# Graph attention, one core: the layer norm's 1/std multiplied in at the projection's eviction, rows centred by VectorE for 24 tiles, and nodes added to stored results in the tail

## The chip, the cores and the metric

One Trainium2 chip, one of its cores. The time is that of one launch on the device, in microseconds. Times inside the program come from one profiled execution and are counted from its first instruction.

## What is computed

`x` has 6144 nodes of 512 features, `adj` is a 6144 x 6144 matrix of 0 and 1 (int32), thinly filled. There are 8 heads of 64 features.

```python
h = maximum(layernorm(x), 0)              # (x - mean) / sqrt(var + 1e-5), no weights
g = einsum('ni,hif->hnf', h, W)           # projection, 8 heads
s1, s2 = einsum('hnf,hf->hn', g, a1), einsum('hnf,hf->hn', g, a2)
scores = leaky_relu(s1[:, :, None] + s2[:, None, :], 0.2)
scores = where(adj > 0, scores, -9e15)
att = softmax(scores, -1)
out = x + elu(transpose(einsum('hnm,hmf->hnf', att, g)))
```

## The kernel before

The nodes are cut into 48 tiles of 128. There are two stages, each a block in which every engine runs its own list of instructions, tied by semaphores.

**Stage 1, `project_and_scan` (L496, up to about 340 us).** Per tile t: VectorE takes the moments of the row (`moments`, L559, bn_stats), GpSimd adds them up (`spread`, L724), ScalarE takes the square root (`deviation`, L637), VectorE the reciprocal (`scale`, L564), GpSimd makes the shift (`offset`, L737), and ScalarE writes relu(x / std + shift) in one ACTIVATE (`norm`, L642, L647). TensorE transposes it (`turn`, L684), ScalarE copies the transpose out of PSUM (`turned`, L650), TensorE multiplies with W and the folded score weights (`project`, L693), and ScalarE copies the three results out (`h_out`, L656, L661 to L663). SP stores the finished rows in a table in DRAM and loads the next x rows (six buffers) and adjacency rows, all on one queue (L542 to L555). The first 30 adjacency tiles are scanned beside this: each half tile (1.5 MB, `load_adj`, L241, six buffers) is packed by ScalarE (`pack`, L253, 2.9 us), and VectorE looks for the largest entries (L263, L274, L295, L297). The plan `spread_over` (L355) deals the scan's work over the 48 rounds by estimated cost; ScalarE's packs stand in the round before VectorE's first step of their tile, mostly two in a round. ScalarE's order in round t is: `turned(t)`, `norm(t + 1)`, the first pack, `h_out(t - 1)`, `deviation(t + 3)`, the other packs. TensorE's is `turn(t + 1)`, `project(t)`. VectorE's is `moments(t + 3)`, `scale(t + 2)`, then its scan. `normed` and `normedT` have two buffers.

SP also copies x into the output for tiles 0 to 21, two tiles (512 KB) at a time, in rounds 2 to 22 (`copy_nodes`, L215, L220): 11 DMAs from DRAM to DRAM.

**Stage 2, `attend_edges` (L768).** 33 units (one or two tiles, or a part of one), in 29 groups that end in a result. GpSimd gathers table rows by index (L904, L909), 6 to 10 indirect DMAs of 128 rows per unit, up to three units ahead of VectorE (`AHEAD`) and as a ring of 36 row buffers allows. VectorE scores the edges (`score_edges`, L1136, the first step is L1141), ScalarE takes the exponential, VectorE weighs the rows (L1156), TensorE adds them up, VectorE normalises (L1168), ScalarE does the negative side of elu (`grow`, L965), VectorE finishes it (`finish`, L1173). The last 18 adjacency tiles are scanned beside units 0 to 18. `result` has four buffers.

What happens to a finished result depends on its tile. Groups 0 to 15 (tiles 0 to 21) "lie in the output": GpSimd adds them to the copied x by an accumulating DMA from SBUF to DRAM (`add_x`, L888), issued after the gathers of the unit four later. Groups of tiles 22 to 43 get x added in SBUF by an accumulating DMA (L890), and ScalarE stores them (`store`, L973, L979), four units later. For the last four tiles x is loaded beforehand, VectorE adds it, and SP stores.

## Time and profile before

| | us |
|---|---|
| Three runs | 772.21, 772.41, 775.91; median 772.41 |
| The profiled execution | 777.28 |
| Its span, first to last instruction | 775.6 |
| Busy: TensorE / VectorE / ScalarE / GpSimd | 575.2 / 651.3 / 477.7 / 422.4 |
| DMA moved | 269.50 MB, mean 347 GB/s |

The profiled execution is a single one and lies 4.9 us above the median of the three runs; shares and durations are read from it. Engines in the rows: PE is TensorE's matmuls, PEld its weight loads, DVE is VectorE, ACT ScalarE, POOL GpSimd, SP SyncE; a q behind a name is the engine's queue. In the rows some tiles bear another tile's name, since they lend its memory: `nodes` stands for `h_rows` and for half of the adjacency buffers.

### The profile page before, as it was taken

The numbers are of one execution on the slowest core, as the hardware profiler recorded it, in microseconds if no ns is written. First come the engines' busy times: TensorE is split into PE (matmuls) and PEld (weight loads), VectorE is DVE, ScalarE is ACT, GpSimd is POOL, SyncE is SP. The second block draws the span as 40 slices with busy tenths as digits, with TensorE's granted clock in tenths as the row PEclk, the third lists the DMA queues.
The fourth block names the chain that finished last, engine by engine and source line by source line (L and its number), as shares of the span: only waits on it lengthen the run. The fifth ranks groups of instructions, "written<-read, shape, count | busy, mean of one in ns | idle before, by whom it ended". The sixth has DMA issues, their size and how long they took to land.

```text
span 775.6 us, 9118 instructions
## 1 busy us (share of the span) xinstructions
PE 575.2 (74%) x2184; PEld 408.2 (53%) x2184; DVE 651.3 (84%) x1966; ACT 477.7 (62%) x763; POOL 422.4 (54%) x805
## 2 busy tenths in 40 slices
PE   0479798898888788683767868685777659988672
PEld 0245454554444445353556657474656448776561
DVE  4659979899976776775879999999989988999983
ACT  0678977799898989925645666675655223334322
POOL 6634434353333332227766457657756876788850
PEclk9989899999888888875769888877788879999986
DMA  9999999999999999917999999999999887999994
GB/s 287 420 380 388 402 358 382 411 385 419 421 417 391 422 419 419 423 69 229 399 406 417 410 407 398 399 393 407 402 393 354 216 219 176 229 245 281 307 243 157
DMA packets 62395, 269.50 MB, mean 347 GB/s; under 512 B 12050, under 2 KB 12050, under 8 KB 49876
## 3 DMA queue, kind: packets, MB, share of 16 engines
q1 hardware_dynamic: 33520, 185.81, 59.5%
q0 software_dynamic: 25824, 77.31, 32.8%
q10 hardware_dynamic: 2996, 5.77, 2.0%
q8 instruction: 19, 0.31, 0.2%
q14 instruction: 36, 0.29, 0.1%
HBM read 243.49 MB, written 31.13 MB: 354 GB/s over the span
## 4 chain that ended last, share of the span: by engine, by line
DVE 21%; DMA 11%; POOL 10%; issue 8%; ACT 3%; PE 2%; DVEq 0%; ACTq 0%; POOLq 0%
DVE nodes L1156 9%; DMA nodes<-table,list_column 9%; POOL nodes L909 5%; POOL nodes L904 4%; DVE agg L1168 3%; DVE places L274 2%; ACT result L970 2%; DMA nodes<-table,column 2%; ACT result L972 2%; DVE best L263 1%; DVE to_row L1132 1%; DMA out_dram<-result 1%; DVE result L1176 1%; DVE owner L1097 0%; PE psC L1315 0%
## 5 line engine op out<-in xcount | busy, mean ns | idle before, releaser
L698 PE MATMUL psH<-sb_W,normedT 128*128 128x512 f32 x384 | 231.7, 695 | 0.0
L253 ACT ACTIVATE packed<-adj_rows,eight 128x3072 uint8<-128x3072 int32 x66 | 188.7, 2860 | 0.8
L904 POOL DMA_INDIRECT nodes<-table,column x138 | 137.4, 995 | 68.3 <-issue 39.9
L749 POOL TENSOR_TENSOR nodes<-nodes 128x520 f32<-128x520 f32 x47 | 60.9, 1296 | 154.2 <-ACT nodes L663 154.2
L1331 PE MATMUL psP<-nodes,ident 128*128 128x256 f32 x276 | 105.5, 471 | 50.4 <-issue 43.8
L909 POOL DMA_INDIRECT nodes<-table,list_column x109 | 110.1, 1010 | 57.7 <-issue 29.9
L1156 DVE TENSOR_TENSOR nodes<-nodes,psW 128x2048 f32<-128x2048 f32 (+4 forms) x66 | 138.7, 2141 | 0.0
L699 PEld LDWEIGHTS psS<-sb_Wa,normedT 128*128 128x128 f32 x384 | 80.5, 210 | 107.1 <-issue 107.1
L274 DVE FIND_INDEX8 places<-best,packed 128x8 uint32<-128x96 f32 (+6 forms) x240 | 109.9, 466 | 0.0
L263 DVE MAX8 best<-packed 128x8 f32<-128x96 f32 (+6 forms) x240 | 102.7, 459 | 6.4 <-ACT packed L253 6.4
L1332 PE MATMUL psP<-nodes,ident 128*128 128x264 f32 x276 | 102.1, 458 | 0.0
L1331 PEld LDWEIGHTS psP<-nodes,ident 128*128 128x128 f32 x276 | 61.6, 235 | 65.0 <-issue 49.8
L690 PE MATMUL psT<-ident,normed 128*128 128x128 f32 x192 | 35.7, 316 | 74.9 <-ACT normed L647 74.9
L253 ACT ACTIVATE packed<-nodes,eight 128x3072 uint8<-128x3072 int32 x30 | 86.4, 2881 | 0.1
L970 ACT ACTIVATE result<-agg 128x1024 f32<-128x1024 f32 (+1 forms) x29 | 26.4, 909 | 84.3 <-DVE agg L1168 78.4
L1338 PE MATMUL psP<-nodes,to_row 128*128 128x256 f32 x218 | 72.1, 415 | 8.0 <-DVE nodes L1156 8.0
L1332 PEld LDWEIGHTS psP<-nodes,ident 128*128 128x128 f32 x276 | 64.7, 234 | 12.6
L1339 PE MATMUL psP<-nodes,to_row 128*128 128x264 f32 x218 | 71.3, 411 | 0.0
L698 PEld LDWEIGHTS psH<-sb_W,normedT 128*128 128x128 f32 x384 | 66.1, 216 | 0.0
L690 PEld LDWEIGHTS psT<-ident,normed 128*128 128x128 f32 x192 | 24.5, 164 | 77.9 <-ACT normed L647 77.9
L699 PE MATMUL psS<-sb_Wa,normedT 128*128 128x16 f32 x384 | 60.0, 232 | 0.0
L1338 PEld LDWEIGHTS psP<-nodes,to_row 128*128 128x128 f32 x218 | 45.0, 210 | 20.0 <-DVE nodes L1156 11.6
(182 smaller groups left out, 882.6 us busy)
## 6 DMA issues: line engine op xcount, KB each, us to landing
adj_rows<-in_adj_dram SPq DMA_DIRECT2D x66, 1536.0 KB, 10.2
nodes<-in_adj_dram SPq DMA_DIRECT2D x30, 1536.0 KB, 12.7
table<-nodes SPq DMA_DIRECT2D x48, 260.0 KB, 8.8
sb_x_rows<-in_x_dram SPq DMA_DIRECT2D x48, 256.0 KB, 9.1
out_dram<-in_x_dram SPq DMA_DIRECT2D x11, 512.0 KB, 11.3
result<-in_x_dram POOLq DMA_DIRECT2D x11, 512.0 KB, 7.9
out_dram<-result ACTq DMA_DIRECT2D x11, 512.0 KB, 4.6
out_dram<-result POOLq DMA_DIRECT2D x6, 512.0 KB, 6.5
```

The source lines that it names most:

```text
L253: nc.scalar.activation(words.bitcast(mybir.dt.uint8), sb["adj_rows"][buffer_of(i)][:], ACT.Square, bias=sb["eight"][:], scale=-17.0, accum ...
L263: ins = nc.vector.max(sb["best"][:, t % 2, 8 * n:8 * n + 8], sb["packed"][:, t % 2, lo:hi])
L274: ins = nc.vector.max_index(sb["places"][:, t % 2, 8 * n:8 * n + 8], sb["best"][:, t % 2, 8 * n:8 * n + 8], sb["packed"][:, t % 2, lo:hi])
L698: nc.tensor.matmul(psH[:, t % 2], normedT[:, t % 2, kc], sb["W"][:, kc], start=(kc == 0), stop=(kc == KC - 1))
L699: mm = nc.tensor.matmul(psS[:, t % 2, 0:2 * H], normedT[:, t % 2, kc], sb["Wa"][:, kc], start=(kc == 0), stop=(kc == KC - 1))
L904: nc.gpsimd.indirect_dma_start(out=nodes[:, node_at[u] + i * w.direct + j], out_offset=None, in_=table, in_offset=bass.IndirectOffsetOnAxi ...
L909: nc.gpsimd.indirect_dma_start(out=nodes[:, node_at[u] + w.directs + q], out_offset=None, in_=table, in_offset=bass.IndirectOffsetOnAxis(a ...
L1156: nc.vector.tensor_tensor(rows, rows, psW[:, lo:hi].unsqueeze(3).to_broadcast([P, hi - lo, H, F]), ALU.mult).then_inc(weighted, 1)
L1331: nc.tensor.matmul(low, sb["ident"][:], nodes[:, n, 0:LOW], start=a, stop=False)
L1332: nc.tensor.matmul(high, sb["ident"][:], nodes[:, n, LOW:TABLE], start=a, stop=False)
L1338: nc.tensor.matmul(low, to_row[:, u % TURNS, r], nodes[:, n, 0:LOW], start=False, stop=z)
L1339: mm = nc.tensor.matmul(high, to_row[:, u % TURNS, r], nodes[:, n, LOW:TABLE], start=False, stop=z)
```

## The change

The norm is split. The shift becomes minus the mean (GpSimd, straight from the moments), rows are only centred and clipped, `relu(x - mean)`, and 1/std, which is positive, is multiplied in per row when the projection leaves PSUM: a scale operand on each of the three copies of `h_out`. So `offset` and its two GpSimd operations per tile turn into one that needs no std. ScalarE centres tiles 0 to 23 (now with one per-partition operand); VectorE centres tiles 24 to 47 with a tensor_scalar (`lift`), in its own round before.

The 11 copies of x into the output in stage 1 are gone. Results of groups 0 to 15 are stored by ScalarE as they are; in units 21 to 31 GpSimd issues 11 accumulating DMAs from x to the output, two tiles each, in 128 pieces of 4096 bytes.

```diff
+ADDED_LAST = 22
+ON_ACT = TILES // 2
...
         def _(sp):
...
-                    sp.wait_ge(norm_done, t + 1)
+                    normed_by(sp, t)
                     sp.dma_start(x_rows[:, t % XB], x[(t + XB) * P:(t + XB + 1) * P]).then_inc(x_loaded[t % XB], 16)
...
-                if t % 2 == 0 and 1 <= t // 2 <= len(COPIED):
-                    copy_nodes(sp, sb, x, out, COPIED[t // 2 - 1])
...
+            def lift(t):
+
+                if ON_ACT <= t < TILES:
+                    dve.wait_ge(shift_done, t + 1)
+                    dve.wait_ge(transposed, t - 1)
+                    nc.vector.tensor_scalar(normed[:, t % 2], x_rows[:, t % XB], shift[:, t:t + 1], 0.0, ALU.add, ALU.max).then_inc(lifted, 1)
...
             for t in range(TILES):
                 moments(t + 3)
-                scale(t + 2)
+                scale(t)
+                lift(t + 1)
...
             def norm(t):
-                if t < TILES:
+                if t < ON_ACT:
...
-                    nc.scalar.activation(normed[:, t % 2], x_rows[:, t % XB], ACT.Relu, bias=shift[:, t:t + 1],
-                                         scale=rstd[:, t:t + 1]).then_inc(norm_done, 1)
+                    nc.scalar.activation(normed[:, t % 2], x_rows[:, t % XB], ACT.Relu, bias=shift[:, t:t + 1]).then_inc(norm_done, 1)
...
-                nc.scalar.activation(h_rows[:, t % HB, 0:HF], psH[:, t % 2], ACT.Copy)
-                nc.scalar.activation(sb["s12"][:, :, t], psS[:, t % 2, 0:2 * H].rearrange("p (a h) -> p a h", a=2), ACT.Copy)
-                nc.scalar.activation(h_rows[:, t % HB, HF:TABLE], psS[:, t % 2, H:2 * H], ACT.Copy).then_inc(h_copied, 1)
+                act.wait_ge(rstd_done, t + 1)
+                nc.scalar.activation(h_rows[:, t % HB, 0:HF], psH[:, t % 2], ACT.Copy, scale=rstd[:, t:t + 1])
+                nc.scalar.activation(sb["s12"][:, :, t], psS[:, t % 2, 0:2 * H].rearrange("p (a h) -> p a h", a=2), ACT.Copy, scale=rstd[:, t:t + 1])
+                nc.scalar.activation(h_rows[:, t % HB, HF:TABLE], psS[:, t % 2, H:2 * H], ACT.Copy, scale=rstd[:, t:t + 1]).then_inc(h_copied, 1)
...
                 pool.wait_ge(moment_step, 4 * t + 2)
+                nc.gpsimd.tensor_tensor(shift[:, t:t + 1], both[:, t, 1:2], minus_half[:], ALU.mult).then_inc(shift_done, 1)
...
-            def offset(t):
-                if t >= TILES:
-                    return
-                pool.wait_ge(rstd_done, t + 1)
-                nc.gpsimd.tensor_tensor(scaled[:, t:t + 1], both[:, t, 1:2], rstd[:, t:t + 1], ALU.mult).then_inc(scaled_done, 1)
-                pool.wait_ge(scaled_done, t + 1)
-                nc.gpsimd.tensor_tensor(shift[:, t:t + 1], scaled[:, t:t + 1], minus_half[:], ALU.mult).then_inc(shift_done, 1)
...
             def add_x(g):
 
                 w, o = GROUPED[g], g % 4
-                if kept(w):
+                if kept(w) or added_last(w):
                     return
                 pool.wait_ge(bent, g + 1)
-                if lies_in_output(w):
-                    if g == 0:
-                        pool.wait_ge(sb["copied"], 16 * len(COPIED))
-                    nc.gpsimd.dma_start(ot[:, w.tile:w.tile + w.tiles], result[:, o, 0:w.tiles], accum_op=ALU.add).then_inc(laid[o], 16)
-                else:
-                    nc.gpsimd.dma_start(result[:, o, 0:w.tiles], xt[:, w.tile:w.tile + w.tiles], accum_op=ALU.add).then_inc(x_added[o], 16)
+                nc.gpsimd.dma_start(result[:, o, 0:w.tiles], xt[:, w.tile:w.tile + w.tiles], accum_op=ALU.add).then_inc(x_added[o], 16)
+
+            def add_to_stored(t):
+
+                for g, w in enumerate(GROUPED):
+                    if t <= w.tile < t + PAIR_TILES:
+                        pool.wait_ge(stored[g % 4], out_written(g))
+                rows = slice(t * P, (t + PAIR_TILES) * P)
+                nc.gpsimd.dma_start(out[rows].rearrange("(p r) d -> p (r d)", r=PAIR_ROWS),
+                                    x[rows].rearrange("(p r) d -> p (r d)", r=PAIR_ROWS), accum_op=ALU.add, max_dma_last_dim=4096).then_inc(laid, 16)
...
                 if u >= 4 and UNITS[u - 4].last:
                     add_x(UNITS[u - 4].group)
+                if 0 <= u - (U - 1 - PAIRS) < PAIRS:
+                    add_to_stored(PAIR_TILES * (u - (U - 1 - PAIRS)))
...
                 if g >= 4:
-                    act.wait_ge(laid[o] if lies_in_output(GROUPED[g - 4]) else stored[o], out_written(g - 4))
+                    act.wait_ge(stored[o], out_written(g - 4))
...
-                act.wait_ge(x_added[g % 4], out_written(g))
+                if added_last(w):
+                    act.wait_ge(bent, g + 1)
+                else:
+                    act.wait_ge(x_added[g % 4], nodes_added(g))
                 act.dma_start(ot[:, w.tile:w.tile + w.tiles], result[:, g % 4, 0:w.tiles]).then_inc(stored[g % 4], 16)
```

`added_last(w)` is true for units of tiles below 22, `PAIRS` is 11, U is 33, and SP waits at the end for all stores and all 11 additions.

## Rows read from the trace of the kernel before

**Rows 1.** The page, part 1: busy time, share of the span, instructions.

```profile
PE 575.2 (74%) x2184; PEld 408.2 (53%) x2184; DVE 651.3 (84%) x1966; ACT 477.7 (62%) x763; POOL 422.4 (54%) x805
```

**Rows 2.** Table by stage: length, busy us (instructions) per engine, TensorE clock, DMA share, GB/s.

```profile
41.00:170.00 129.00, 115.16 (x445) 67.84 (x446) 112.65 (x549) 104.33 (x180) 56.96 (x176) 0.92 0.98 384
170.00:330.00 160.00, 131.36 (x462) 76.43 (x462) 125.29 (x456) 148.85 (x210) 56.70 (x173) 0.86 1.01 417
410.00:600.00 190.00, 141.47 (x542) 114.42 (x541) 183.24 (x460) 117.30 (x171) 121.79 (x123) 0.82 1.03 398
660.00:756.00 96.00, 76.86 (x329) 63.83 (x329) 87.82 (x153) 32.80 (x81) 72.40 (x67) 0.92 0.97 261
```

**Rows 3.** Line L241, adjacency loads on SP's queue: all of them, then three moments.

```profile
DMA to landing us min/median/max: 6.6/11.1/24.2
...
L241 SPq DMA_DIRECT2D nodes<-in_adj_dram x1: 487/487/487, 90.3 to 90.3; - x1
DMA to landing us min/median/max: 12.5/12.5/12.5
...
L241 SPq DMA_DIRECT2D nodes<-in_adj_dram x2: 327/552/777, 166.9 to 168.2; - x2
DMA to landing us min/median/max: 9.2/10.4/11.6
...
L241 SPq DMA_DIRECT2D nodes<-in_adj_dram x1: 328/328/328, 305.0 to 305.0; - x1
DMA to landing us min/median/max: 16.8/16.8/16.8
```

**Rows 4.** Timeline of ScalarE: start, length, line, operation, tiles (loads 16, 28, 59).

```profile
127.57 2.87 ACT L253 ACTIVATE packed<-nodes,eight 128x3072 uint8<-128x3072 int32 x1
...
188.90 2.84 ACT L253 ACTIVATE packed<-nodes,eight 128x3072 uint8<-128x3072 int32 x1
...
324.69 2.98 ACT L253 ACTIVATE packed<-nodes,eight 128x3072 uint8<-128x3072 int32 x1
```

**Rows 5.** Timeline of GpSimd in the tail; in brackets its idle time before.

```profile
647.96 1.07 POOL L904 DMA_INDIRECT nodes<-table,column  x1 [3.85 <-PE psP L1339]
...
679.29 1.37 POOL L890 DMA_DIRECT2D result<-in_x_dram  x1
680.97 1.45 POOL L904 DMA_INDIRECT nodes<-table,column  x1 [0.30 <-issue]
...
737.14 1.06 POOL L904 DMA_INDIRECT nodes<-table,column  x1 [0.30 <-issue]
```

**Rows 6.** Timeline of VectorE, the last unit's score.

```profile
748.58 0.21 DVE L1141 TENSOR_TENSOR score<-nodes,sides 128x48 f32<-128x48 f32 x1 [0.51 <-DMA nodes<-table,list_column]
```

**Rows 7.** Timeline of ScalarE in one round of the first stage.

```profile
92.76 0.81 ACT L647 ACTIVATE normed<-sb_x_rows,shift,rstd 128x512 f32<-128x512 f32 x1
93.47 0.60 ACT L661 ACTIVATE nodes<-psH 128x512 f32<-128x512 f32 x1
93.94 0.19 ACT L662 ACTIVATE s<-psS 128x16 f32<-128x16 f32 x1
```

**Rows 8.** VectorE: line L1097 from 342 to 350, and L562 from 170 to 330.

```profile
L1097 DVE TENSOR_SCALAR owner<-owner,half_sq x4: 401/404/406, 342.7 to 344.5; 128x384 f32<-128x384 f32 x4
...
L562 DVE BATCH_NORM_STATS2 stats<-sb_x_rows 128x6 f32<-128x512 f32 x21 | 14.3, 683 | 7.6 <-DMA sb_x_rows<-in_x_dram 7.6
```

**Rows 9.** DMA queues from 40 to 200: packets, MB, share of 16 engines.

```profile
q1 hardware_dynamic: 11880, 62.43, 98.6%
```

**Rows 10.** Timeline of VectorE, the score of unit 15.

```profile
567.78 0.24 DVE L1141 TENSOR_TENSOR score<-nodes,sides 128x80 f32<-128x80 f32 x1 [2.03 <-DMA nodes<-table,list_column]
```

**Rows 11.** Line L888, GpSimd's accumulates into the output: ns min/median/max.

```profile
L888 POOL DMA_DIRECT2D out_dram<-result x16: 1015/1030/1382, 437.9 to 658.1; - x16
```

**Rows 12.** GpSimd's DMA queue from 375 to 430, and from 437 to 600.

```profile
q0 software_dynamic: 2957, 9.84, 46.4%
...
q0 software_dynamic: 9533, 29.19, 50.6%
```

More of the change, by code:

```diff
@@ L48 @@
 HALF = N // 2
-COPY_TILES, COPY_ROWS = 2, 8
+PAIR_TILES, PAIR_ROWS = 2, 2
 HB = 3
-COPIED = tuple(range(0, 22, COPY_TILES))
+ADDED_LAST = 22
 KEPT = 4
+ON_ACT = TILES // 2
 PACK = 4
@@ L214, in cut_count, with added_last @@
     return sum(steps_of(s) for s in range(1, t))
-def copy_nodes(queue, sb, x, out, t):
-    rows = slice(t * P, (t + COPY_TILES) * P)
-    queue.dma_start(out[rows].rearrange("(p r) d -> p (r d)", r=COPY_ROWS),
-                    x[rows].rearrange("(p r) d -> p (r d)", r=COPY_ROWS)).then_inc(sb["copied"], 16)
-def lies_in_output(unit):
-    return all(t - t % COPY_TILES in COPIED for t in range(unit.tile, unit.tile + unit.tiles))
+def added_last(unit):
+    return unit.tile + unit.tiles <= ADDED_LAST
 def kept(unit):
@@ L524, in project_and_scan @@
         weight_of_gap, minus_half, eps = buf("weight_of_gap", [P, 1]), buf("minus_half", [P, 1]), buf("eps", [P, 1])
-        squares, std, rstd, scaled, shift = (buf(n, [P, TILES]) for n in ("squares", "std", "rstd", "scaled", "shift"))
+        squares, std, rstd, shift = (buf(n, [P, TILES]) for n in ("squares", "std", "rstd", "shift"))
         normed, normedT, h_rows = buf("normed", [P, 2, D]), buf("normedT", [P, 2, KC, P]), sb["h_rows"]
@@ L532, in project_and_scan @@
         stats_done, moment_step, squares_done, std_done = sem("stats_done"), sem("moment_step"), sem("squares_done"), sem("std_done")
-        rstd_done, scaled_done, shift_done, norm_done = sem("rstd_done"), sem("scaled_done"), sem("shift_done"), sem("norm_done")
+        rstd_done, shift_done, norm_done, lifted = sem("rstd_done"), sem("shift_done"), sem("norm_done"), sem("lifted")
         transposed, normedT_done, projected = sem("transposed"), sem("normedT_done"), sem("projected")
@@ L538, in project_and_scan, with normed_by @@
         block = ctx.enter_context(nc.Block())
+        def normed_by(engine, t):
+            if t < ON_ACT:
+                engine.wait_ge(norm_done, t + 1)
+            else:
+                engine.wait_ge(lifted, t - ON_ACT + 1)
         @block.sync
@@ L642, in norm @@
             def norm(t):
-                if t < TILES:
+                if t < ON_ACT:
                     act.wait_ge(shift_done, t + 1)
@@ L685, in turn @@
                 if t < TILES:
-                    pe.wait_ge(norm_done, t + 1)
+                    normed_by(pe, t)
                     if t >= 2:
@@ L752, in _ @@
                 spread(t)
-            offset(0)
-            offset(1)
             for t in range(TILES):
                 spread(t + 3)
-                offset(t + 2)
                 if t >= 1:
@@ L831, in attend_edges @@
         gathered = [sem(f"gathered{u}") for u in range(AHEAD)]
-        x_added, stored, laid = ([sem(f"{n}{u}") for u in range(4)] for n in ("x_added", "out_stored", "out_added"))
+        x_added, stored = ([sem(f"{n}{u}") for u in range(4)] for n in ("x_added", "out_stored"))
+        laid = sem("nodes_laid")
+        PAIRS = ADDED_LAST // PAIR_TILES
         squared, owners, looked_up, facts_done = sem("squared"), sem("owners"), sem("looked_up"), sem("facts_done")
@@ L846, in out_written, with nodes_added @@
         def out_written(g):
-            return 16 * sum(lies_in_output(v) == lies_in_output(GROUPED[g]) for v in GROUPED[g % 4:g + 1:4])
+            return 16 * len(GROUPED[g % 4:g + 1:4])
+        def nodes_added(g):
+            return 16 * sum(not added_last(v) for v in GROUPED[g % 4:g + 1:4])
         owned = [sum(w.n for w in UNITS[:u]) for u in range(U + 1)]
@@ L929, in _ @@
             for k in range(4):
-                sp.wait_ge(stored[k], 16 * sum(not lies_in_output(w) for w in GROUPED[k::4]))
-                sp.wait_ge(laid[k], 16 * sum(lies_in_output(w) for w in GROUPED[k::4]))
+                sp.wait_ge(stored[k], 16 * len(GROUPED[k::4]))
+            sp.wait_ge(laid, 16 * PAIRS)
         @block.scalar
@@ L973, in store @@
             def store(u):
-                if u < 0 or not UNITS[u].last or lies_in_output(UNITS[u]) or kept(UNITS[u]):
+                if u < 0 or not UNITS[u].last or kept(UNITS[u]):
                     return
                 g, w = UNITS[u].group, UNITS[u]
-                act.wait_ge(x_added[g % 4], out_written(g))
+                if added_last(w):
+                    act.wait_ge(bent, g + 1)
+                else:
+                    act.wait_ge(x_added[g % 4], nodes_added(g))
                 act.dma_start(ot[:, w.tile:w.tile + w.tiles], result[:, g % 4, 0:w.tiles]).then_inc(stored[g % 4], 16)
```

3 lines of the change are left out of this document (removed).

## The prediction

> **What bounds the kernel now.** I read the page's busy row first [rows 1]: VectorE is busy 84% of the span, no engine is at 95%, so the span has to be taken apart. The table by stage does that [rows 2]. From 41 to 330 us (layer norm and projection beside the scan of the first 30 adjacency tiles) the sixteen DMA engines are busy 98 to 101% of the time; in the second half of it (170 to 330) ScalarE is busy 148.9 of 160 us, VectorE 125.3. From 410 to 600 VectorE is busy 183.2 of 190 us and DMA 103%. From 660 to 756 (the last ten units, no adjacency left) the DMA share is still 97% while only 261 GB/s move: it is gathers and accumulates that fill it. So the question is, stage by stage, which of two full resources ends last.
>
> In the first stage the adjacency loads tell. Loads 28 and 29 (half tiles) are issued at 166.9 and 168.2 us and land 9.2 and 11.6 us later, at 176.1 and 179.8; ScalarE packs load 28 only at 188.90, 12.8 us after landing. Load 59, the last that this stage packs, is issued at 305.0, lands 16.8 us later at 321.8, and is packed at 324.69, 2.9 us after landing [rows 3, 4]. So ScalarE still sets the pace, but the loads are slower than it: 145.7 us between the two landings against 135.8 between the two packs, and the stock of landed rows is nearly eaten up at the end. Earlier it was ample: load 16 lands 12.5 us after 90.3 and is packed at 127.57, 24.8 us later [rows 3, 4].
>
> In the tail GpSimd tells. It issues gathers three units ahead of VectorE. It last waits for a free buffer at 647.96 (3.85 us, for TensorE) [rows 5]. After that it issues without a rest, 0.30 us between two [rows 5], while VectorE stays busy 87.8 of 96 us [rows 2]; at 748.58, its last unit, VectorE idles 0.51 us for the gathers [rows 6]. GpSimd's lead is used up exactly at the end.
>
> **Part 1, one over std at the eviction.** The norm loses one per-partition operand, the three copies out of PSUM gain one each. The pitch on ScalarE is read from start to start, as neighbours overlap: the norm (two such operands) takes 93.47 - 92.76 = 0.71 us, the 512-wide copy without one 93.94 - 93.47 = 0.47 [rows 7]. If the norm's extra 0.24 us is due to its operands, one is worth 0.12; if it is due to reading SBUF, an operand is worth nothing. Bounds 0 and 0.12; I take 0.11, since the source makes little sense as a cost for the same width. Per tile then +3 x 0.11 - 0.11 = +0.22 us in the tiles where ScalarE still norms. Load 28 is issued in round 22, so 22 x 0.22 = 4.8 us, less where ScalarE waits for TensorE anyway (it is busy 104.3 of 129 us there [rows 2]): +4 us at load 28's issue.
>
> The Trainium skill, ScalarE: Activation LUTs, section "What ACT_TABLE_LOAD costs", says that each pointer operand of one value per partition adds about 93 ns to an ACTIVATE. By that rule the operand and not the source is the cause, and the first half loses 22 x 2 x 0.093 = 4.1 us; by the other end of my bounds it would lose nothing. This speaks against the change where TensorE's input still comes from ScalarE.
>
> The reciprocal leaves the chain from statistics to norm, and two GpSimd operations per tile with it. GpSimd is busy 56.7 of 160 us, VectorE's waits for std turn into running ahead: worth nothing on the path, as it is ScalarE's pitch that counts.
>
> **Part 2, VectorE centres tiles 24 to 47.** ScalarE loses 0.71 and gains 0.33 us: -0.38 x 24 = -9.1 us. VectorE gains 24 tensor_scalar of 128x512; the nearest row, the same operation at 128x384, takes 0.40 us [rows 8], so 0.5 each, 12 us in a stage where it has 35 us free. It stands behind bn_stats of tile t+3, which waited 7.6 us in all for x rows in this stretch [rows 8]; while that wait lasts the lift and with it TensorE's transpose is late. I price this at 0 to 3 us, take 0: the lift comes a round ahead.
>
> **Part 3, the copies go.** Eleven copies of 0.524 MB on SP's queue. From 40 to 200 us that queue takes 98.6% of 160 us for 62.43 MB, 2.53 us per MB [rows 9]. So they hold 5.77 x 2.53 = 14.6 us of DMA time, all of it before 180 us, where landed rows lie unused for over 12 us; SP issues eleven fewer DMAs and waits for ScalarE anyway. They buy a shorter queue: load 28 would land about 6.6 us after its issue, the shortest landing of any [rows 3], in place of 9.2, so -2.6 us.
>
> **Stage 1 together.** Load 28 lands at 166.9 + 4 + 6.6 = 177.5. From there DMA is full, the transfers up to load 59 stand in the same order in the same queue, and take up to 145.7 us: landing 323.2, or 2 to 4 us sooner if the gaps between close (taken: 321). ScalarE alone would reach this pack at 324.7 + 4 - 9.1 = 319.6, so it now waits for the load: **the gain of part 2 is cut off by the loads**. With about 1 us less behind the last pack (TensorE's transposes are done early): -3.5 us. Bounds: 0 and -8.
>
> **Part 4, the accumulates into the output go (groups 0 to 15).** VectorE idles 2.03 us before the score of unit 15 at 567.78, for gathers that queue behind such accumulates; the two next waits of the kind I count at 0.5 us [rows 10]. Elsewhere from 410 to 600 VectorE is the limit. Their GpSimd time (1.03 us the small ones, 1.38 the large [rows 11]) lies beside it. ScalarE issues 16 more stores; it is busy 117 of 190 us, and what it waits for there, the end of finish, is four units old. -2.5 us, bounds 0 and -4.
>
> **Part 5, eleven accumulates DRAM to DRAM in units 21 to 31.** On GpSimd, a 512 KB accumulate costs 680.97 - 679.29 - 0.30 = 1.38 us [rows 5]; one of 128 pieces (256 KB before) 1.03 [rows 11]. The new one has 128 pieces of 4 KB: 1.03. In units 21 to 23 it takes the place of an old one; the lead gained in units 18 to 20 is lost at the wait of 647.96. In units 24 to 31 it is added: 8 x 1.03 - 0.35 = **+8 us**, all of it on the path at unit 32, since the lead there is zero. Its own wait (stores of ten units before) is over when reached.
>
> On the DMA engines: gathers cost 46.4% of 55 us for 9.84 MB, 2.59 us per MB, so a unit of six (1.60 MB) 4.1 us. From 437 to 600 the queue has 29.19 MB in 82.5 us; 3.15 MB of it are accumulates, the rest at 2.59 leaves them 4.8 us per MB, 2.5 us per 512 KB [rows 12]. A plain store at 2.53 us per MB [rows 9] is 1.3 us. A unit now needs 4.1 + 2.5 + 1.3 = 7.9 us of DMA per 9.3 us of GpSimd (from 680.97 to 737.14 it passes six units of six gathers and an accumulate in 56.2 us [rows 5]); at the 97% of the stage's row it is nearer 9. The new accumulate adds between 1.3 (a plain transfer) and 5 (both ends in DRAM); nearest are the accumulates, 2.5. Then 11.5 us stand against GpSimd's 9.3 + 1.03 = 10.3: about 0.7 to 1.2 us of backlog per unit for eight units, **+5 us** (0 to +30).
>
> The Trainium skill, DMA: Bandwidth & Descriptors, section "Anatomy of one DMA — SWDGE (gpsimd) path", fits a DMA of GpSimd as 2.0 us + bytes / 436e3. By that a 524 KB transfer holds the engines 1.2 us, no backlog arises, and the tail would cost 8 us and not 13; the fit makes no difference for an accumulate, and the rows above do.
>
> **Sum:** -3.5 - 2.5 + 8 + 5 = +7 us. The profiled execution took 777.3 us (span 775.6); the median of the runs is 772.4, 0.6% lower. The difference is carried over: 772.4 + 7 = **779.4 us**. A change under 0.5% (3.9 us: 768.5 to 776.3) can't be told from none.
>
> **Rivals.**
> (a) Only GpSimd's time counts in the tail, no DMA backlog: -3.5 - 2.5 + 8 = +2, 774.4 us. For it: only 261 GB/s there [rows 2]. Against: the 97% of the same row. Chance 0.22.
> (b) Faster: DMA sets the pace of the whole first stage, so that the 14.6 us of the copies come off in full, and ScalarE's relief lets it use them: -14.6 - 2.5 + 8 = -9, 763.3 us. For it: 98 to 101% DMA from 41 to 330. Against: a landed load lay 24.8 us in its buffer while the copies ran [rows 3, 4]. It decides where load 59 lands: before about 312 us this case holds. Chance 0.20.
> (c) An accumulate between two DRAM tensors costs 5 us of the engines: 14 against 10.3 us per unit, +30 in the tail, 796 us. Chance 0.10.
> (d) The change doesn't relieve ScalarE: the lift comes late behind VectorE's scan, TensorE waits, stage 1 gains nothing: 783 us. Chance 0.05.
> The forecast has 0.43; a sixth of it (backlog small) lies within 0.5%.
>
> **Numbers.** Slower by over 0.5%: forecast 0.36 + (c), (d) 0.15 = 0.51; within: 0.07 + (a) = 0.29; faster: (b), 0.20. The range leaves out the lower half of (b) and (c): 764 to 790. The forecast's own range is 775 to 786.
>
> **What would show it.** Right: load 59 packed the moment it lands, ScalarE idle for DMA near 320; the three evictions with a pitch 0.1 us longer each; from unit 27 on VectorE idle for gathers at each score, 8 us and more in all; landing times of the tail's gathers over 6 us. Wrong: load 59 landing near 312; no idle VectorE after 700; a first stage over 8 us shorter.

## The result, and the profile after

The kernel with the change takes 781.06 us, median of 16 runs (777.62 to 783.61). The kernel before, run beside it on the same chip, takes 775.81, median of 16 (769.03 to 778.73). The ratio is **1.0085, interval 1.0063 to 1.0107: slower by 0.85%**. Between the medians lie 5.25 us, 0.68%; the ratio isn't their quotient. Predicted were +7 us on 772.4, which is 0.9%. One thing has to be known of the runs: of the 92 of the kernel before that were timed beside the experiments and have their mean granted TensorE clock on record, 65 have 0.854 or more of full speed and a median of 773.0 us, 27 have less and a median of 778.6, while after's 16 runs all have 0.855 or more, so that against the upper group the change costs 8.1 us (the line at 0.854 was drawn after the runs).

The profiled execution took 778.8 us, its span 777.0. The busy row of its page answers to [rows 1], the table by stage (same stretches, same columns) to [rows 2]:

```profile
PE 570.7 (73%) x2184; PEld 406.2 (52%) x2184; DVE 659.5 (85%) x1990; ACT 472.3 (61%) x739; POOL 406.8 (52%) x752
```

```profile
41.00:170.00 129.00, 112.24 (x441) 66.28 (x442) 112.11 (x547) 108.40 (x175) 53.25 (x154) 0.93 0.90 345
170.00:330.00 160.00, 128.66 (x475) 74.14 (x475) 138.29 (x497) 140.93 (x190) 57.71 (x150) 0.91 1.01 416
410.00:600.00 190.00, 142.05 (x537) 115.32 (x538) 186.41 (x465) 117.14 (x172) 110.02 (x115) 0.82 0.99 394
660.00:756.00 96.00, 73.10 (x289) 59.25 (x287) 77.66 (x142) 31.09 (x73) 72.50 (x69) 0.86 1.05 299
```

The work moved as the change says: in the second stretch VectorE has 13 us more and ScalarE 7.9 us less than in [rows 2]; in the first the DMA share fell from 98 to 90% (345 GB/s), so part of the copies' time now lies idle. But the last stretch, with no more computation than before, has 10 us less VectorE in it: 77.7 of 96 us against 87.8. VectorE stands still there.

VectorE's scores of the last nine units (timeline of VectorE; in brackets its idle time just before and what ended it):

```profile
672.21 0.22 DVE L1151 TENSOR_TENSOR score<-nodes,sides 128x64 f32<-128x64 f32 x1
...
709.48 0.21 DVE L1151 TENSOR_TENSOR score<-nodes,sides 128x48 f32<-128x48 f32 x1 [0.69 <-DMA nodes<-table,list_column]
719.68 0.21 DVE L1151 TENSOR_TENSOR score<-nodes,sides 128x48 f32<-128x48 f32 x1 [2.09 <-DMA nodes<-table,list_column]
730.00 0.21 DVE L1151 TENSOR_TENSOR score<-nodes,sides 128x48 f32<-128x48 f32 x1 [2.20 <-DMA nodes<-table,list_column]
741.02 0.21 DVE L1151 TENSOR_TENSOR score<-nodes,sides 128x48 f32<-128x48 f32 x1 [4.00 <-DMA nodes<-table,list_column]
751.94 0.21 DVE L1151 TENSOR_TENSOR score<-nodes,sides 128x48 f32<-128x48 f32 x1 [4.27 <-DMA nodes<-table,list_column]
```

Before, the last unit's wait was 0.51 us [rows 6]; now there are five waits, 13.25 us together, each for gathers. (A unit's first score is shown; the units are counted u0 to u32.)

As runs of one kernel differ, both kernels were profiled a second time (below). The table puts the same moments of all traces side by side. "Load 59" is when the last adjacency load that the first stage packs lands; "eviction" is the start of tile 47's 512-wide copy out of PSUM, the end of the first stage's chain; u0, u3, u17, u24, u32 are the starts of those units' scores. The first five columns are moments, in us from the first instruction; the last four are lengths in us.

| kernel | load 28 issued | load 59 | its pack | eviction | u0 | u3 to u17 | u24 to u32 | after u32 | span |
|---|---|---|---|---|---|---|---|---|---|
| before | 166.9 | 321.8 | 324.7 | 339.6 | 365.7 | 190.1 | 69.8 | 27.1 | 775.6 |
| before, again | 163.0 | 318.9 | 320.5 | 334.0 | 360.3 | 189.9 | 70.1 | 27.2 | 771.4 |
| after | 167.3 | 320.8 | 321.8 | 335.9 | 361.6 | 187.2 | 79.7 | 25.0 | 777.0 |
| after, again | 168.8 | 320.9 | 322.0 | 334.4 | 361.8 | 187.2 | 81.0 | 26.6 | 779.5 |
| compute_alone | 170.2 | 323.5 | 324.5 | 336.9 | 362.8 | 193.6 | 69.7 | 26.2 | 774.0 |
| nodes_alone | 164.6 | 317.1 | 318.8 | 332.3 | 357.5 | 187.2 | 79.7 | 25.5 | 774.5 |
| thin_pairs | 167.2 | 320.9 | 321.9 | 334.3 | 361.2 | 187.1 | 77.1 | 25.4 | 774.4 |
| no_pairs | 169.7 | 322.2 | 323.2 | 335.6 | 361.7 | 188.3 | 69.9 | 27.2 | 771.1 |
| plain_evictions | 163.5 | 315.8 | 315.8 | 330.0 | 356.7 | 188.3 | 80.8 | 26.7 | 774.0 |
| all_on_act | 170.3 | 321.4 | 323.8 | 337.2 | 364.1 | 187.9 | 80.7 | 26.3 | 782.4 |
| pairs_sooner | 168.7 | 321.5 | 322.5 | 336.6 | 361.0 | 196.8 | 71.1 | 26.4 | 779.0 |
| twelve_sooner | 170.2 | 323.0 | 324.0 | 336.4 | 364.2 | 193.7 | 70.1 | 27.7 | 775.7 |
| copies_back | 169.4 | 323.2 | 324.3 | 338.4 | 363.9 | 188.2 | 80.4 | 25.9 | 781.3 |
| nodes_ten | 164.1 | 317.2 | 318.8 | 332.3 | 359.2 | 187.6 | 70.8 | 26.2 | 765.6 |

### The profile page after: what moved, and what is told of

Read it like the earlier page. It is cut to its first block, busy times and chain, and to the rows that moved or that the text cites. A ratio compares the mean times of both kernels' runs of the same rounds, so it can differ in the third digit from the quotient of the medians.

```text
span 777.0 us, 9120 instructions
## 1 busy us (share of the span) xinstructions
PE 570.7 (73%) x2184; PEld 406.2 (52%) x2184; DVE 659.5 (85%) x1990; ACT 472.3 (61%) x739; POOL 406.8 (52%) x752
## 4 chain that ended last, share of the span: by engine, by line
DVE 20%; POOL 15%; issue 9%; DMA 5%; PE 5%; ACT 1%; DVEq 0%; POOLq 0%
DVE nodes L1166 7%; POOL nodes L909 7%; POOL nodes L914 7%; DMA nodes<-table,list_column 4%; DVE places L268 3%; DVE best L257 2%; DMA nodes<-table,column 2%; PE psP L1341 2%; POOL result L886 1%; PE psP L1342 1%; DVE agg L1178 1%; POOL out_dram L894 1%; DVE to_row L1142 1%; PE psP L1349 1%; DVE result L1186 1%
## 5 line engine op out<-in xcount | busy, mean ns | idle before, releaser
L703 PE MATMUL psH<-sb_W,normedT 128*128 128x512 f32 x384 | 223.8, 674 | 13.0 <-ACT normedT L658 13.0
L909 POOL DMA_INDIRECT nodes<-table,column x138 | 135.5, 982 | 72.0 <-issue 39.9
L1341 PE MATMUL psP<-nodes,ident 128*128 128x256 f32 x276 | 108.2, 481 | 54.8 <-issue 41.5
L914 POOL DMA_INDIRECT nodes<-table,list_column x109 | 108.3, 994 | 67.1 <-DVE list_column L1131 37.0
L704 PEld LDWEIGHTS psS<-sb_Wa,normedT 128*128 128x128 f32 x384 | 78.2, 204 | 101.9 <-issue 101.9
L1342 PE MATMUL psP<-nodes,ident 128*128 128x264 f32 x276 | 105.3, 470 | 0.0
L1341 PEld LDWEIGHTS psP<-nodes,ident 128*128 128x128 f32 x276 | 63.2, 241 | 69.7 <-issue 54.1
L695 PE MATMUL psT<-ident,normed 128*128 128x128 f32 x192 | 34.1, 305 | 68.0 <-ACT normed L652 49.6
L977 ACT ACTIVATE result<-agg 128x1024 f32<-128x1024 f32 (+1 forms) x29 | 26.4, 909 | 88.1 <-DVE agg L1178 57.3
L1342 PEld LDWEIGHTS psP<-nodes,ident 128*128 128x128 f32 x276 | 66.3, 240 | 13.2
L703 PEld LDWEIGHTS psH<-sb_W,normedT 128*128 128x128 f32 x384 | 63.4, 207 | 15.1 <-ACT normedT L658 15.1
## 6 DMA issues: line engine op xcount, KB each, us to landing
nodes<-in_adj_dram SPq DMA_DIRECT2D x30, 1536.0 KB, 14.6
```

What stands on the lines that cost most here:

```text
L703: nc.tensor.matmul(psH[:, t % 2], normedT[:, t % 2, kc], sb["W"][:, kc], start=(kc == 0), stop=(kc == KC - 1))
L704: mm = nc.tensor.matmul(psS[:, t % 2, 0:2 * H], normedT[:, t % 2, kc], sb["Wa"][:, kc], start=(kc == 0), stop=(kc == KC - 1))
L909: nc.gpsimd.indirect_dma_start(out=nodes[:, node_at[u] + i * w.direct + j], out_offset=None, in_=table, in_offset=bass.IndirectOffsetOnAxi ...
L914: nc.gpsimd.indirect_dma_start(out=nodes[:, node_at[u] + w.directs + q], out_offset=None, in_=table, in_offset=bass.IndirectOffsetOnAxis(a ...
L1341: nc.tensor.matmul(low, sb["ident"][:], nodes[:, n, 0:LOW], start=a, stop=False)
L1342: nc.tensor.matmul(high, sb["ident"][:], nodes[:, n, LOW:TABLE], start=a, stop=False)
```

## The experiments

The question after the result: is the loss the tail's alone, how much of it is GpSimd's issuing and how much the DMA engines, and what became of the first stage's gain.

### The two halves apart: compute_alone and nodes_alone

compute_alone is the kernel before with the new split norm and nothing else: the copies and the old accumulates stay. nodes_alone is the other half.

```diff
 # compute_alone: project_and_scan as after, and in it still
+                if t % 2 == 0 and 1 <= t // 2 <= len(COPIED):
+                    copy_nodes(sp, sb, x, out, COPIED[t // 2 - 1])
 # nodes_alone: attend_edges as after; project_and_scan as before, less
-                if t % 2 == 0 and 1 <= t // 2 <= len(COPIED):
-                    copy_nodes(sp, sb, x, out, COPIED[t // 2 - 1])
```

> The kernel before with the compute part of the change alone: 1/std at the evictions, rows centred by VectorE from tile 24 on; the copies of x and the accumulates into the output stay. Forecast's theory (the adjacency loads cut ScalarE's gain off): load 28 lands near 180 us, since the evictions slow the first half by 4 us and the copies still stand in the queue; the last pack of stage 1 waits for its load and ends within 2 us of where it ended before; ratio to before 0.998 to 1.003. Rival (ScalarE's relief counts in full): the last pack 5 us sooner, ratio 0.993.

Measured: 776.79 us, ratio 1.0013 (0.9979 to 1.0047). The tail u24 to u32 is 69.7 us, as before. VectorE waits 3.42 us at unit 15, as the old accumulates still stand there (2.03 before, [rows 10]). The middle takes 193.6 us, 3.6 more than before: besides unit 15 there is a wait of 2.96 us for gathers at unit 6, and no run settles where it comes from. The first stage ends at 336.9, between the two profiles of before, and load 28 lands at 180.3, as expected.

> The change's handling of x alone (no copies in stage 1, plain stores of groups 0 to 15, 11 accumulates DRAM to DRAM in units 21 to 31), with the layer norm as before. Forecast's theory: stage 1 unchanged within 1 us (ScalarE's pace), the middle 3 us shorter, the tail 11 to 13 us longer; ratio 1.010 to 1.013. Rival (b), the copies' 14.6 us of DMA time come off the first stage: ratio 0.993 to 0.998.

Measured: 778.70 us, ratio 1.0054 (1.0016 to 1.0092). The tail takes 79.7 us, all of the change's; the middle 187.2, as in after. **The expectation missed in the first stage:** it ends at 332.3, earlier than in either profile of before, where I had expected no gain from the copies alone. The whole ratio came out lower than expected, by this and by a tail 1 to 3 us shorter than said. What the copies are worth is taken up below. What follows: the tail's loss is the nodes' half by itself. The arithmetic's half shows no difference clear of noise over all runs, but that hides two things: compute_alone's 12 runs all have a granted clock of 0.857 or more, and against the runs of before with 0.854 or more its 776.8 us are 3.8 us slower; what it wins is that the lower clock, which 27 of 92 runs of before show, doesn't occur in it.

### GpSimd or the DMA engines: thin_pairs and no_pairs

thin_pairs issues the same 11 accumulates with the same 128 pieces each, but of 512 bytes instead of 4096, so most of x is not added to the first 22 tiles. GpSimd's work stays, the bytes go. no_pairs issues none of them; those tiles stay without x.

```diff
 # thin_pairs
-                nc.gpsimd.dma_start(out[rows].rearrange("(p r) d -> p (r d)", r=PAIR_ROWS),
-                                    x[rows].rearrange("(p r) d -> p (r d)", r=PAIR_ROWS), accum_op=ALU.add, max_dma_last_dim=4096).then_inc(laid, 16)
+                nc.gpsimd.dma_start(out[rows].rearrange("(p r) d -> p (r d)", r=PAIR_ROWS)[:, 0:128],
+                                    x[rows].rearrange("(p r) d -> p (r d)", r=PAIR_ROWS)[:, 0:128], accum_op=ALU.add).then_inc(laid, 16)
 # no_pairs
-                if 0 <= u - (U - 1 - PAIRS) < PAIRS:
-                    add_to_stored(PAIR_TILES * (u - (U - 1 - PAIRS)))
```

> The changed kernel with each of the 11 accumulates cut to 512 bytes in each of its 128 pieces (x is added to an eighth of tiles 0 to 21 only): GpSimd's work is the same, the DMA engines' about an eighth. Forecast's theory (8 us of GpSimd, 3 to 5 us of DMA backlog): 3 to 5 us faster than the changed kernel, ratio to before 1.002 to 1.005, gathers of units 28 to 32 land about 5 us after issue and not 8. Rival (a), only GpSimd's time counts: as the changed kernel, ratio 1.008.

Measured: 778.37 us, ratio 1.0024 (0.9992 to 1.0056); tail 77.1 us.

> The changed kernel without the 11 accumulates (x isn't added to tiles 0 to 21). Forecast's theory: the whole cost of the tail goes, 11 to 13 us less than the changed kernel, ratio to before 0.992 to 0.995; no idle VectorE over 0.5 us before a score after unit 3. If the tail were lost to the plain stores by ScalarE or to something else, the ratio stays over 1.0.

Measured: 770.37 us, ratio 0.9952 (0.9924 to 0.9980), 10.7 us less than after; tail 69.9 us, as before. A wait of 1.14 us at unit 15 is left where none over 0.5 was expected.

Three kernels take the tail apart. Before and no_pairs: 70 us. With the issues but hardly any bytes: 77.1. With the bytes: 79.7 and 81.0, mean 80.35. So **of 10.4 us, 7.1 to 7.2 are GpSimd's issuing and 3.2 the transfers**. The split is good to about 1 us, as thin_pairs has one profile and after's two tails lie 1.3 us apart. How the bytes act is seen in the DMA issues from 700 to 760 (tiles, queue, count, KB each where there are any, median us from issue to landing), first of before, then after, then thin_pairs:

```profile
q0 software_dynamic: 4655, 12.45, 82.4%
...
nodes<-table,column POOLq DMA_INDIRECT x20, 5.6
nodes<-table,list_column POOLq DMA_INDIRECT x10, 5.4
```

```profile
q0 software_dynamic: 5049, 14.30, 90.2%
...
out_dram<-in_x_dram POOLq DMA_DIRECT2D x4, 512.0 KB, 12.1
nodes<-table,column POOLq DMA_INDIRECT x16, 9.6
nodes<-table,list_column POOLq DMA_INDIRECT x10, 8.2
```

```profile
nodes<-table,column POOLq DMA_INDIRECT x18, 5.4
out_dram<-in_x_dram POOLq DMA_DIRECT2D x4, 64.0 KB, 7.8
nodes<-table,list_column POOLq DMA_INDIRECT x10, 4.0
```

A gather lands 9.6 us after its issue in place of 5.6; thin_pairs brings it back to 5.4. This is the backlog, and it goes with the bytes. And in thin_pairs VectorE still idles for gathers, though they land quickly (timeline of VectorE, the last two scores; the same of no_pairs below it):

```profile
739.52 0.21 DVE L1151 TENSOR_TENSOR score<-nodes,sides 128x48 f32<-128x48 f32 x1 [4.25 <-DMA nodes<-table,list_column]
749.02 0.21 DVE L1151 TENSOR_TENSOR score<-nodes,sides 128x48 f32<-128x48 f32 x1 [2.84 <-DMA nodes<-table,list_column]
```

```profile
735.96 0.21 DVE L1148 TENSOR_TENSOR score<-nodes,sides 128x48 f32<-128x48 f32 x1 [0.90 <-DMA nodes<-table,list_column]
743.94 0.21 DVE L1148 TENSOR_TENSOR score<-nodes,sides 128x48 f32<-128x48 f32 x1 [0.63 <-DMA nodes<-table,list_column]
```

The releaser in the bracket is "DMA" in both, yet the cause in thin_pairs is that the gather was issued late. The landing time beside the wait tells the two apart. The issuing itself (timeline of GpSimd in after):

```profile
671.32 0.95 POOL L914 DMA_INDIRECT nodes<-table,list_column  x1 [0.30 <-issue]
672.27 1.37 POOL L886 DMA_DIRECT2D result<-in_x_dram  x1
673.07 1.51 POOL L894 DMA_DIRECT2D out_dram<-in_x_dram  x1
674.89 1.08 POOL L909 DMA_INDIRECT nodes<-table,column  x1 [0.30 <-issue]
```

From the first accumulate to the next gather 2.62 us pass (2.60 to 2.64 in all eight units, and in thin_pairs too); with one accumulate it was 680.97 - 679.29 = 1.68 [rows 5]. The second costs 0.94, not 1.03, and 8 x 0.94 - 0.35 = 7.2 is what thin_pairs shows in the tail.

### The operand: plain_evictions

```diff
-                nc.scalar.activation(h_rows[:, t % HB, 0:HF], psH[:, t % 2], ACT.Copy, scale=rstd[:, t:t + 1])
+                nc.scalar.activation(h_rows[:, t % HB, 0:HF], psH[:, t % 2], ACT.Copy)
...
```

and the same on the two small copies, so that 1/std isn't applied at all.

> The changed kernel with the scale operand taken off the three evictions (1/std is left out of the projection; their wait for it stays). Theory (each per-partition operand costs ScalarE 0.10 us, 0.3 us per tile, which delays load 28 by some 5 us, and the loads after it set the end of stage 1): load 28 issued 4 to 5 us sooner than in the changed kernel, load 59 lands 4 us sooner, the last eviction 3 to 4 us sooner; ratio to before 1.003 to 1.005. Rival (the eviction's operands are hidden behind TensorE): no difference, 1.008.

Timeline of ScalarE in one round, after:

```profile
94.22 0.77 ACT L652 ACTIVATE normed<-sb_x_rows,shift 128x512 f32<-128x512 f32 x1
94.83 0.74 ACT L666 ACTIVATE nodes<-psH,rstd 128x512 f32<-128x512 f32 x1
95.40 0.33 ACT L667 ACTIVATE s<-psS,rstd 128x16 f32<-128x16 f32 x1
95.55 0.33 ACT L668 ACTIVATE nodes<-psS,rstd 128x8 f32<-128x8 f32 x1
95.70 0.36 ACT L645 ACTIVATE std<-squares,eps 128x1 f32<-128x1 f32 x1
```

and plain_evictions:

```profile
91.70 0.73 ACT L652 ACTIVATE normed<-sb_x_rows,shift 128x512 f32<-128x512 f32 x1
92.31 0.60 ACT L666 ACTIVATE nodes<-psH 128x512 f32<-128x512 f32 x1
92.79 0.20 ACT L667 ACTIVATE s<-psS 128x16 f32<-128x16 f32 x1
92.86 0.20 ACT L668 ACTIVATE nodes<-psS 128x8 f32<-128x8 f32 x1
92.91 0.33 ACT L645 ACTIVATE std<-squares,eps 128x1 f32<-128x1 f32 x1
```

From start to start: the 512-wide copy 0.57 against 0.48 us, the 16-wide 0.15 against 0.07, the 8-wide 0.15 against 0.05. The norm with one operand takes 0.61 in both, with two it took 0.71 [rows 7]. **An operand costs 0.08 to 0.10 us whatever the width**: three more are +0.27, one less in the norm -0.10, so +0.17 us per tile. The Trainium skill, ScalarE: Activation LUTs, section "What ACT_TABLE_LOAD costs", has 93 ns for one; the trace agrees, with these 0.08 to 0.10.

In time: load 28 is issued 3.8 us sooner than in after's first profile, load 59 lands 5.0 sooner and is packed at once, and the stage's last eviction comes 5.9 sooner (5.3, 5.1 and 4.4 against the second). Measured in all: 778.42 us, ratio 1.0055 (1.0022 to 1.0088), a little above the range expected. The medians of after and this kernel differ by 0.3%, and the intervals of their ratios overlap; the tail keeps its loss.

### VectorE's share: all_on_act

`ON_ACT = TILES`: ScalarE centres every tile, VectorE none.

> The changed kernel with all 48 tiles centred by ScalarE (no lift by VectorE). Forecast's theory (the loads cut off what VectorE's help gives): ScalarE's pace alone would bring the last pack 3 to 8 us later than in the changed kernel, ratio to before 1.012 to 1.018, and the last pack comes more than 3 us after its load lands. Rival (VectorE's help is worth nothing since stage 1 is bound by the loads in any case): as the changed kernel, 1.008.

Measured: 786.38 us (six runs), ratio 1.0165 (1.0109 to 1.0220), against 1.0085 (1.0063 to 1.0107) with the lift; the intervals just don't overlap. **The ratio is as expected, the moments are not:** the last pack comes 2.0 us later than in after (said: 3 to 8) and 2.4 us after its load lands (said: more than 3). u0 comes 2.4 us later. In after, the lift (VectorE, 170 to 330: count, busy us, mean ns, idle before) costs what was estimated:

```profile
L561 DVE BATCH_NORM_STATS2 stats<-sb_x_rows 128x6 f32<-128x512 f32 x21 | 14.4, 683 | 16.9 <-DMA sb_x_rows<-in_x_dram 16.8
L573 DVE TENSOR_SCALAR normed<-sb_x_rows,shift 128x512 f32<-128x512 f32 x23 | 11.3, 491 | 0.0
```

0.49 us each. The lift is thus worth having once the operands sit on the evictions. In the waits of the same stretch ScalarE's pack stands still for VectorE's search:

```profile
ACT packed L247 <- DVE places L268: 6.2, 3, 4.8
```

The lift isn't needed for this wait. Its longest, before load 52 is packed, goes back to the wait in the L561 row, of VectorE for x rows, which stand in the same queue as the adjacency loads (timeline of after, 286 to 297):

```profile
294.38 0.69 DVE L561 BATCH_NORM_STATS2 stats<-sb_x_rows 128x6 f32<-128x512 f32 x1 [3.46 <-DMA sb_x_rows<-in_x_dram]
...
296.44 2.85 ACT L247 ACTIVATE packed<-nodes,eight 128x3072 uint8<-128x3072 int32 x1 [4.76 <-DVE places L268]
```

Load 52 itself had landed 7.1 us earlier. The kernel before, which has no lift, shows 4.0 us of idle ScalarE before the same pack in its second profile (below).

### The copies: copies_back

The kernel after, with 11 copies of the old size and at the old places on SP's queue, into a scratch tensor in DRAM that nobody reads.

```diff
+                if t % 2 == 0 and 1 <= t // 2 <= 11:
+                    rows = slice((t - 2) * P, t * P)
+                    sp.dma_start(scratch[rows].rearrange("(p r) d -> p (r d)", r=8),
+                                 x[rows].rearrange("(p r) d -> p (r d)", r=8)).then_inc(sb["copied"], 16)
```

> The changed kernel with 11 copies of x of the old shape put back on SP's queue in rounds 2 to 22, into a scratch tensor. Forecast's theory (the copies hold the queue before load 28, and only 2 to 4 us of their 14.6 reach the end): load 28 lands 3 to 4 us later than in the changed kernel, load 59 too; ratio to before 1.011 to 1.014. Rival (b), they cost the stage their DMA time: 14 us, ratio 1.026.

Measured: 784.57 us (six runs), ratio 1.0158 (1.0097 to 1.0220), above the range expected and 0.7% over after's, though the intervals overlap. In the trace load 28 is issued 1.3 us later than the mean of after's two profiles and lands 1.8 later (said: 3 to 4), load 59 lands 2.3 later, u0 comes 2.2 later. That is about a sixth of the 14.6 us of DMA time that the copies hold, and the ratio's 0.7%, 5.6 us, is still under half of it. That the landed rows which lay unused absorbed the rest fits the traces, but no run shows it by itself. Rival (b), by which all 14.6 us count, falls on it.

### Both kernels again: before_again and after_again

Unchanged kernels, to see what one profile is worth.

> The kernel before once more, to see how far stage 1, the middle and the tail vary from one profiled execution to the next: the end of stage 1 within 3 us of 339.6, the tail from unit 24 to unit 32 within 1 us of 69.8.

Measured: 772.99 us. Its first stage ends at 334.0, **5.6 us before that of the same kernel's other profile**, where at most 3 were expected; behind u3 the two agree within 0.3 us in each column of the table. Table by stage, 170 to 330, to be held against the second row of [rows 2]:

```profile
170.00:330.00 160.00, 125.34 (x466) 73.58 (x466) 127.19 (x471) 146.98 (x208) 56.86 (x172) 0.91 1.00 413
```

TensorE's granted clock is 0.91 in place of 0.86. And VectorE waits 23.2 us for x rows, where it was 7.6 [rows 8] (VectorE, 170 to 330):

```profile
L562 DVE BATCH_NORM_STATS2 stats<-sb_x_rows 128x6 f32<-128x512 f32 x21 | 14.4, 685 | 23.2 <-DMA sb_x_rows<-in_x_dram 23.2
```

ScalarE's timeline shows the packs of loads 52 and 59; between them is the last load, L241 at 300 us (the landing times are of two loads, this one has the longest):

```profile
294.10 2.86 ACT L253 ACTIVATE packed<-nodes,eight 128x3072 uint8<-128x3072 int32 x1 [4.04 <-issue]
```

```profile
L241 SPq DMA_DIRECT2D nodes<-in_adj_dram x1: 328/328/328, 300.7 to 300.7; - x1
...
DMA to landing us min/median/max: 17.5/17.8/18.2
```

```profile
320.49 2.93 ACT L253 ACTIVATE packed<-nodes,eight 128x3072 uint8<-128x3072 int32 x1
```

300.7 + 18.2 = 318.9: packed 1.6 us after landing. ScalarE has no idle time over 0.3 us between these two packs, and none in after between the same two: in neither is it the load that the last pack waits for.

> The changed kernel once more, for the same: the end of stage 1 within 3 us of 335.9, the tail from unit 24 to unit 32 within 1 us of 79.7; the difference of the tails, 10 us, repeats, while single spans may lie 3 us apart.

Measured: 781.23 us. Its first stage is that of after (load 59 at 320.9, u0 at 361.8), its tail 1.3 us longer, where at most 1 was expected. The difference of the tails, 10 us and more, repeats, also in the four other kernels that keep the 11 accumulates as they are (nodes_alone, plain_evictions, all_on_act, copies_back: 79.7 to 80.8 us).

### The adds sooner: pairs_sooner, twelve_sooner, nodes_ten

If GpSimd's lead decides, the same accumulates should cost nothing ahead of GpSimd's last wait for a buffer, which resets the lead [rows 5].

```diff
 # pairs_sooner
+PAIR_UNITS = (13, 15, 17, 19, 21, 22, 23, 24, 25, 26, 27)
-                if 0 <= u - (U - 1 - PAIRS) < PAIRS:
-                    add_to_stored(PAIR_TILES * (u - (U - 1 - PAIRS)))
+                if u in PAIR_UNITS[:PAIRS]:
+                    add_to_stored(PAIR_TILES * PAIR_UNITS.index(u))
 # twelve_sooner: the same, and
-ADDED_LAST = 22
+ADDED_LAST = 12
 # nodes_ten: nodes_alone (norm as before), and
+ADDED_LAST = 10
+PAIR_UNITS = (18, 19, 20, 21, 22)
```

> The changed kernel with its 11 accumulates issued in units 13, 15, 17, 19, 21 to 27 in place of 21 to 31, so four stand in units 24 to 31 and not eight. Theory (each accumulate behind the last wait of GpSimd costs the tail its 1.03 us and some DMA time, before it nothing): 4 to 6 us faster than the changed kernel, ratio to before 1.001 to 1.004. Rival (the accumulates cost DMA time wherever they stand): unchanged, 1.008.

Measured: 779.20 us, ratio 1.0049 (1.0019 to 1.0079), **a miss by a little** (said: up to 1.004), and its interval overlaps after's. The tail is healed, 71.1 us, but the middle takes 196.8 in place of 187.2. Two waits make up these 9.6 us, 2.58 us at unit 6, ahead of all accumulates, and this one (timeline of VectorE):

```profile
569.28 0.24 DVE L1152 TENSOR_TENSOR score<-nodes,sides 128x80 f32<-128x80 f32 x1 [7.02 <-DMA nodes<-table,list_column]
```

The larger one is of gathers behind an accumulate while adjacency loads still fill the engines: the loss of [rows 10], made larger.

> As pairs_sooner, but for tiles 0 to 11 alone: six accumulates in units 13, 15, 17, 19, 21 and 22; tiles 12 to 21 are treated as the later ones (x added in SBUF, then stored). Theory: no new work of GpSimd behind unit 23, so the tail is as before, stage 1 and most of the middle keep their gain: ratio to before 0.992 to 0.996. Rival (the tail's loss comes from the stores or from DMA load in the middle): over 1.0.

Measured: 777.12 us, ratio 1.0037 (1.0010 to 1.0065). **Missed:** 0.4% slower than before, not faster. The tail is as expected (70.1), but the middle takes 193.7: three accumulates still lie in units 13, 15 and 17 (a wait of 3.83 us at unit 15), and 2.63 us are lost at unit 6, ahead of them, as in compute_alone. And the first stage, with the dear evictions, ends at 336.4, between before's two profiles.

nodes_ten draws the conclusion from both: nothing before unit 18, nothing behind unit 22, no copies, and the norm left as it was. The tiles between are added in SBUF.

> The change's handling of x for tiles 0 to 9 alone, with the layer norm as before: no copies in stage 1, plain stores of groups 0 to 9, five accumulates DRAM to DRAM in units 18 to 22; tiles 10 to 43 get x added in SBUF. Theory: units 18 to 22 have no adjacency loads beside them any more and GpSimd waits 4 us at unit 23 anyway, so the five accumulates (5 x 1.03 us) cost 1 us at most; the tail from unit 24 to 32 is 70 us as before; stage 1 ends 2 to 5 us sooner without copies and without the dearer evictions: ratio to before 0.993 to 0.997. Rival (an accumulate costs its time wherever it stands, or the copies were free): 1.0 or more.

Measured: **769.70 us against 773.23, ratio 0.9951 (0.9915 to 0.9987), faster than both kernels, by 0.5% than before.** Its trace has the middle at 187.6, the tail at 70.8, and the eviction at 332.3. The last two scores of the timeline:

```profile
730.16 0.21 DVE L1149 TENSOR_TENSOR score<-nodes,sides 128x48 f32<-128x48 f32 x1 [0.58 <-DMA nodes<-table,list_column]
739.34 0.21 DVE L1149 TENSOR_TENSOR score<-nodes,sides 128x48 f32<-128x48 f32 x1 [1.50 <-DMA nodes<-table,list_column]
```

2.1 us of waiting are left of 13.25.

## Why the prediction held, and where its steps did not

The balance of the two pairs of profiles (mean of two each): up to u0 -1.3 us, u0 to u3 -0.7, u3 to u17 -2.8, u17 to u24 +0.3, u24 to u32 +10.4, behind it -1.3. Before rounding the sum is +4.7; the mean spans are 778.25 and 773.5. Predicted: +7.

- **Tail, +13 predicted, +10.4 measured.** GpSimd's term was 8 and is 7.2 (0.94 us per issue in place of 1.03). The backlog was 5 and is 3.2: less than the 0.7 to 1.2 us per unit I had, 0.4. The order was right: GpSimd first, DMA on top of it. It kills rival (a), by which no backlog arises; thin_pairs minus after is that backlog. Here belongs the other rule weighed: by an estimate from the fit in the Trainium skill, DMA: Bandwidth & Descriptors, section "Anatomy of one DMA — SWDGE (gpsimd) path", there would be none, and the trace disagrees, by 3.2 us and by gathers landing in 9.6 us. Rival (c), 30 us, is excluded.
- **Middle, -2.5 predicted, -2.8 measured.** The wait at unit 15 is gone in both profiles of after.
- **Behind the last score, nothing predicted, -1.3 measured**, with 1.6 us between after's two profiles; no run settles it.
- **First stage, -3.5 predicted; between -4.1 and +1.5 measured** (u0 of after's profiles, 361.6 and 361.8, against 365.7 and 360.3 of before's). The parts have nearly the sizes they were given. Operands cost +0.17 us per tile (taken: 0.22); load 28 is issued 3.7 us later than in nodes_alone and nodes_ten, which have the old norm and no copies either (taken: 4); the lift costs 0.49 us (taken: 0.5); the copies are worth 1.8 us at load 28's landing (taken: 2.6); behind the last pack, where ScalarE waits for TensorE, 0.9 us are gained (taken: 1).
- **What failed is the step "ScalarE still sets the pace, but the loads are slower than it", with its end, "it now waits for the load".** The step was read from one profile, in which load 59 is packed 2.9 us behind its landing and VectorE waits 7.6 us in all for x rows from 170 to 330. In the other profile of the kernel before VectorE waits 23.2 us for them, ScalarE stands 4.0 us before load 52's pack, so by these waits the queue holds the engines up already, as it does in after (16.8 and 4.8 us). Against that profile the relief of ScalarE won nothing: u0 comes 1.3 to 1.5 us later. And the DMA engines act at another place than forecast: ScalarE doesn't stand idle before the last pack, but waits 25 us earlier for VectorE, which waits for x rows behind the adjacency loads. As forecast, DMA cuts the gain off; there was less of it to cut.
- **The level, and luck.** 7 us were put on 772.4, which lies in the upper clock group of the kernel before, and against this group the change costs 8.1 us (781.06 against 772.99); against all runs beside after it is 5.25. That the total comes near 7 is in part luck, since errors cancel: by the means of the profiles the first stage came out 2.2 us dearer than forecast, the tail 2.6 cheaper, and 2.0 us fell off from u0 to u3 and behind the last score, where nothing had been predicted. The tail's two causes and their order were no luck.
- **The prediction's arithmetic** has three slips, none of which decides anything. From 324.7 to 321 and 1 us more is -4.7, not the -3.5 that it puts down. Eight times 0.7 us, its lowest backlog, is 5.6, not 5. Rival (c) has 30 us on top of GpSimd's 8, which gives 804 us and not 796.
- Of the signs named beforehand, load 59 is packed 1.0 us after its landing (said: the moment it lands), and ScalarE's idle time for DMA near 320 isn't there; the pitches are longer by 0.1 us, VectorE idles for gathers from unit 28 on (said: 27) for 13.25 us (said: 8 and more), and gathers land in 9.6 us (said: over 6).

Open: nodes_alone and nodes_ten end the first stage at 332.3, both without the copies and with the old norm; before's second profile ends it at 334.0. How much of the 1.7 us is the copies and how much the scatter between executions isn't settled, as each is one profile.

## What to carry to other kernels

Look for the engine's last wait before the end: work added ahead of it can be paid from slack, as nodes_ten's five accumulates are (pairs_sooner shows the limit: not where loads still fill the DMA engines); work added behind it is paid in full, however idle the engine looks on the page (GpSimd is 52% busy here, and 0.94 us per unit cost 7 us). Moving transfers out of a stage whose loads have a stock of landed data gains a fraction of their time (2.2 of 14.6 us in the trace), so they must go where they cost less than that. When an operand is moved from one instruction to three small ones, it is paid three times, since its price doesn't depend on the width. And before a step of a few us is read from one profile, take a second: here the two differ by 5.6 us in one stage.
